# A decoder kernel: forget gate first, state space table on two engines, POOL's low angles before its high ones

## The reference

```
feat = x @ W_in; V, Q, F = split(feat)              # block 1, a gated recurrence over the 2 batches
V, Q = gelu(V), gelu(Q); lam = lb + (1 - lb) * sigmoid(F); K = 1 - lam
S_t = lam_t * S_(t-1) + K_t (x) V_t;  o_t = Q_t . S_t
x = layernorm(x + o @ W_out)
scores = (x @ Wq)(ctx @ Wk)^T / sqrt(32), 4 heads   # block 2
attn = softmax over the 32 largest of 154 scores;   c = mean over heads(attn) @ (ctx @ Wv)
u = layernorm(x) * (1 + g*scale_in(c)) + g*shift_in(c)
y = u convolved with K_l = 2 Re sum_n dC_n exp(dtA_n * l), l = 0..511   # s4d
y = y * (1 + g*scale_out(c)) + g*shift_out(c); h = x + y; h += ffn(layernorm(h)); layernorm
```

## Time and profile before

| | us |
|---|---|
| median of three runs | 663.56 (663.29 to 664.49) |
| the profiled execution, its own time | 663.11 |
| its span | 661.3 |
| PE busy | 603.2 (91%) |
| DVE busy | 439.0 (66%) |
| ACT busy | 287.9 (44%) |
| POOL busy | 246.5 (37%) |

### The profile page before, as it was taken

One profiled execution on the slowest core, in us unless ns is written; L12 is line 12 of the kernel. 1 busy time (PEld: TensorE's weight loads), 2 busy tenths in 40 slices (PEclk: granted clock), 3 DMA queues, 4 the chain that ended last, 5 costly groups with the idle time before them and its releaser, 6 DMA issues.

```text
span 661.3 us, 8811 instructions
## 1 busy us (share of the span) xinstructions
PE 603.2 (91%) x3171; PEld 302.0 (46%) x3172; DVE 439.0 (66%) x1173; ACT 287.9 (44%) x548; POOL 246.5 (37%) x179
## 2 busy tenths in 40 slices
PE   8864959998997999999999998999977999999997
PEld 4432548886572332222222442233622345556566
DVE  6899998556559846766776569668645675333335
ACT  7979968213230554444444333534232334221210
POOL 2899271422531344655465344557334100000001
PEclk9955879999999899999999999999979999999999
DMA  8300006021000000000000000000600000000001
GB/s 321 110 0 0 2 1 256 1 68 60 1 0 1 0 0 1 0 1 1 0 1 0 1 1 0 1 0 1 268 22 1 0 1 0 1 1 0 1 0 33
DMA packets 4945, 19.25 MB, mean 29 GB/s; under 512 B 2053, under 2 KB 3462, under 8 KB 4390
## 3 DMA queue, kind: packets, MB, share of 16 engines
q1 hardware_dynamic: 4902, 18.69, 7.5%
HBM read 18.16 MB, written 0.52 MB: 28 GB/s over the span
## 4 chain that ended last, share of the span: by engine, by line
PE 71%; DVE 14%; ACT 7%; POOL 4%; issue 4%; DMA 0%; POOLq 0%; DVEq 0%; ACTq 0%
PE PS L2401 11%; PE PS L1606 9%; PE PS L1622 8%; PE PS L2422 6%; PE PS L1564 5%; PE PS L1590 3%; PE PS L1692 2%; PE PS L1636 2%; PE PS L1609 2%; DVE SB L1853 2%; DVE SB L199 2%; PE PS L2091 2%; POOL SB L238 2%; ACT SB L468 1%; DVE SB L212 1%
## 5 line engine op out<-in xcount | busy, mean ns | idle before, releaser
L1853 DVE TENSOR_REDUCE SB<-PS 128x2 f32<-128x1024 f32 x64 | 78.4, 1226 | 62.9 <-PE PS L1590 62.8
L1839 POOL TENSOR_TENSOR SB<-SB 128x1024 f32<-128x1024 f32 x32 | 75.2, 2352 | 108.7 <-ACT SB L1791 107.8
L1791 ACT ACTIVATE SB<-PS 128x1024 f32<-128x1024 f32 x64 | 65.6, 1024 | 102.3 <-PE PS L1609 102.2
L2401 PE MATMUL PS<-SB 128*128 128x512 f32 x176 | 78.4, 594 | 0.0
L1606 PE MATMUL PS<-SB 64*128 64x512 f32 x256 | 70.4, 627 | 1.1 <-ACT SB L1795 1.1
L1622 PE MATMUL PS<-SB 128*64 128x512 f32 x256 | 67.6, 610 | 0.5 <-DVE SB L1885 0.5
L238 POOL TENSOR_TENSOR SB<-SB 128x4 f32<-128x4 f32 x18 | 19.3, 1073 | 116.9 <-DVE SB L204 104.3
L2460 ACT ACTIVATE SB<-PS 128x512 f32<-128x512 f32 x44 | 26.2, 597 | 80.2 <-PE PS L2401 78.8
L2486 DVE TENSOR_TENSOR SB<-SB,PS 128x512 f32<-128x512 f32 x44 | 30.0, 688 | 41.8 <-PE PS L2401 40.5
L1876 DVE RECIPROCAL SB<-PS 128x256 f32<-128x256 f32 x32 | 55.6, 1744 | 0.0
L2401 PEld LDWEIGHTS PS<-SB 128*128 128x128 f32 x176 | 32.2, 190 | 35.3 <-issue 33.7
(11 more groups left out here) (415 smaller groups left out, 1125.2 us busy)
## 6 DMA issues: line engine op xcount, KB each, us to landing
SB<-exp SPq DMA_DIRECT2D x1, 4352.0 KB, 14.1
SB<-moe SPq DMA_DIRECT2D x1, 4096.0 KB, 14.5
SB<-dft SPq DMA_DIRECT2D x1, 2304.0 KB, 11.6
SB<-att SPq DMA_DIRECT2D x1, 2048.0 KB, 8.2
SB<-mix SPq DMA_DIRECT2D x1, 768.5 KB, 4.4
SB<-mix SPq DMA_DIRECT2D x1, 640.0 KB, 5.5
SB<-ssm SPq DMA_DIRECT2D x1, 602.0 KB, 6.6
SB<-lat SPq DMA_DIRECT2D x1, 585.0 KB
```

Source lines behind the costliest of these rows:

```text
L1791: act.activation(expd[i % 2][:, 1024 * u:1024 * u + 1024], bank(2 * (u % 2), 2), ACT.Exp).then_inc(sem("d_exp"), 1)
L1839: pool.tensor_tensor(half_sums[half], e[:, 0:1024], e[:, 1024:], ALU.add).then_inc(sem("d_half_sum"), 1)
L1853: dve.tensor_reduce(shift[i % 2][:, qt:qt + DK + 1:DK], two_heads(bank(4, 2)), AX_X, ALU.max, negate=True)\
L2401: pe.matmul(bank(2 * (i % 3) + side), w, xsT[:, 512 * n:512 * n + 512], start=True, stop=True).then_inc(sem(("top2_w1", "top2_w3")[side]), 1)
```

## The change

In block 1 PE turns the first half of the stack (phases and rates) ahead of the features, and makes the features of the forget gate first; ACT takes the sigmoid first. DVE starts on the keys as soon as that is there. The table's last part (dC) goes from DVE to POOL as `b_pool_stack`, except the reciprocal; DVE copies the turned first half of the stack and writes eight of the 32 low phases itself. The statistics of the second half stand before the normalisation of the first. POOL's masks and powers come before its film weights. The second half's transposes stand on PE behind `score(0)`, the film inputs behind `score(1)`. The low rounding is in two halves, with `peak(0)` between; the high rounding stands behind the second pair's selection. The memset of 32x1024 is on DVE. POOL makes both low angles, then the marks and film rows, and then the high angles. ACT writes 14 of the 16 high phases behind the film inputs.

The diff, cut to its core:

```diff
--- before.py
+++ after.py
...
-        for m in range(3):
+        pe.wait_ge(sem("s_turns"), 2)
+        for i in range(2):
+            ins = pe.transpose(bank(7)[:, 128 * i:128 * i + 128], stack[:, 128 * i:128 * i + 128], ident)
+        ins.then_inc(sem("s_stack_turned"), 1)
+        for m in (2, 1, 0):
...
+            ins = pe.transpose(bank(7)[:, 128 * i:128 * i + 128], stack[:, 128 * i:128 * i + 128], ident)
+        ins.then_inc(sem("s_stack_turned"), 1)
 
     def a_act(act):
         b_act_stack(act)
         act.wait_ge(sem("a_features"), 2)
-        act.activation(gate_v, bank(0, 2), ACT.Gelu).then_inc(sem("a_gates"), 1)
+        act.activation(forget, bank(4, 2), ACT.Sigmoid, scale=-1.0).then_inc(sem("a_gates"), 1)
         act.wait_ge(sem("a_features"), 4)
         act.activation(gate_q, bank(2, 2), ACT.Gelu).then_inc(sem("a_gates"), 1)
         act.wait_ge(sem("a_features"), 6)
-        act.activation(forget, bank(4, 2), ACT.Sigmoid, scale=-1.0).then_inc(sem("a_gates"), 1)
...
         b_dve_stack(dve, follow)
         dve.wait_ge(sem("mix_in"), 16)
         follow(dve.tensor_scalar(one_less, mix["lower"], -1.0, 1.0, ALU.mult, ALU.add))
-        dve.wait_ge(sem("a_gates"), 3)
-
+        dve.wait_ge(sem("a_gates"), 1)
         follow(dve.tensor_scalar(keys, forget, one_less, None, ALU.mult))
+        follow(dve.scalar_tensor_tensor(carried[:, 0:512], keys[:, 512:], 1.0, keys[:, 0:512], ALU.subtract, ALU.mult))
+        dve.wait_ge(sem("a_gates"), 2)
         for n in range(2):
...
+        variances(0)
+        add(1)
+        spread(1)
+        norm_apply(dve, tiled(xsum), tiled(xs), 0).then_inc(sem("stage_half"), 1)
+        variances(1)
+        norm_apply(dve, tiled(xsum), tiled(xs), 1).then_inc(sem("stage_done"), 1)
 
 
...
+            ins = dve.tensor_copy(s[:, k, :], src)
+        ins.then_inc(sem("s_turns"), 1)
+        Ar, Ai = ssm["A_re"], ssm["A_im"]
+        dve.tensor_tensor(dt_(13), Ar, Ar, ALU.mult)
+        tt(dt_(14), Ai, Ai, ALU.mult)
+        tt(dt_(13), dt_(13), dt_(14), ALU.add)
+        dve.reciprocal(dt_(13), dt_(13)).then_inc(sem("s_dta"), 1)
+        dve.wait_ge(sem("s_stack_turned"), 1)
+        dve.tensor_copy(stack_T[:, 0:256], bank(7)[:, 0:256]).then_inc(sem("s_stack_in"), 1)
+        dve.wait_ge(sem("s_stack_in"), 1)
+        for l in range(LOW_ACT, LOW):
+            ins = dve.tensor_scalar(lag(low_r, LOW)[:, :, l], turn_T, float(l), ssm["quarter"], ALU.mult, ALU.add)
+        follow(ins)
...
+    def b_pool_stack(pool, follow):
+
+        tt = lambda o, a, b, op: pool.tensor_tensor(o, a, b, op)
+        s = stack.rearrange("p (k n) -> p k n", n=N_ST)
+        pool.wait_ge(sem("table_in"), 16)
+        pool.wait_ge(sem("s_trig"), 2)
...
-    def b_dve_rounds(dve):
-
+    def b_dve_low_rounds(dve, h):
+
+        c = slice(2048 * h, 2048 * h + 2048)
         dve.wait_ge(sem("s_low_products"), 1)
-        dve.tensor_scalar(low_k, low_r, MAGIC, MAGIC, ALU.add, ALU.subtract).then_inc(sem("s_rounds"), 1)
+        dve.tensor_scalar(low_k[:, c], low_r[:, c], MAGIC, MAGIC, ALU.add, ALU.subtract).then_inc(sem("s_rounds"), 1)
+
+    def b_dve_high_rounds(dve):
+
         dve.wait_ge(sem("s_high_turns"), 1)
         dve.tensor_scalar(high_t, high_r, MAGIC, MAGIC, ALU.add, ALU.subtract).then_inc(sem("s_rounds"), 1)
...
-        pool.wait_ge(sem("s_rounds"), 2)
+        pool.wait_ge(sem("s_rounds"), 3)
...
-        pool.wait_ge(sem("s_rounds"), 1)
+        pool.wait_ge(sem("s_rounds"), h + 1)
         pool.tensor_tensor(low_k[:, c], low_k[:, c], low_r[:, c], ALU.subtract).then_inc(sem("s_low_products"), 1)
...
+    def b_pe_turn(pe, half):
+
+        pe.wait_ge(sem("x_small_in"), 4)
+        if half == 0:
+            stay_warm(pe, 2, 0, ident)
+        pe.wait_ge(sem(("stage_half", "stage_done")[half]), 1)
+        for t in range(4 * half, 4 * half + 4):
+            ins = pe.transpose(PS[:, 2048 + 128 * t:2048 + 128 * t + 128], tiled(xs)[:, t, :], ident)
+        ins.then_inc(sem(("x_half_turned", "turned")[half]), 1)
+        if half == 0:
...
-        b_act_low_turns(act, 0, 24)
+        act.wait_ge(sem("s_stack_in"), 1)
+        b_act_low_turns(act, 0, 13)
...
-        b_act_low_turns(act, 24, LOW)
-        b_act_high_turns(act, 0, 10)
+        b_act_low_turns(act, 13, 20)
+        b_act_stack_in(act)
         act.wait_ge(sem("x_half_turned"), 1)
         act.activation(xsT[:, 0:512], bank(4), ACT.Copy).then_inc(sem("x_half_in"), 1)
-        b_act_high_turns(act, 10, HIGH)
+        b_act_low_turns(act, 20, LOW_ACT)
+        b_act_high_turns(act, 0, 2)
+
+    def b_act_turned(act):
+
         act.wait_ge(sem("turned"), 1)
...
+        b_pool_stack(pool, follow)
         pool.wait_ge(sem("small_in"), SMALL)
+        follow(pool.tensor_copy(mask_line, ctx_bytes))
+        follow(pool.tensor_scalar(mask_line, mask_line, 1.0, -NEG, ALU.subtract, ALU.mult))
+        by_batch = mask_line.rearrange("p (b g) -> p b g", b=B)
+        m2 = mask_low.rearrange("p (b h g) -> p b h g", b=B, h=2)
+        for h in range(2):
+            pool.tensor_copy(m2[:, :, h, :], by_batch)
+        pool_rstd_half(pool, 0)
+        pool.tensor_copy(ones_low, ones[0:1, :])
+        pool.memset(zeros_low, 0.0).then_inc(sem("masks_in"), 1)
+        pool_rstd_half(pool, 1)
         pool.wait_ge(sem("ssm_in"), 16)
         pool.tensor_scalar(film_w, ssm["W_film"], mod_gate, None, ALU.mult).then_inc(sem("film_w_in"), 1)
         pool.wait_ge(sem("film_w_in"), 1)
...
-        follow(pool.tensor_scalar(text_mask, text_mask, 1.0 / H_X, None, ALU.mult))
-        pool.wait_ge(sem("a_features"), 6)
-        pool.memset(attn1[96:128, :], 1.0).then_inc(sem("x_clear"), 1)
-        pool.wait_ge(sem("x_clear"), 2)
+        pool.tensor_scalar(text_mask, text_mask, 1.0 / H_X, None, ALU.mult).then_inc(sem("masks_in"), 1)
+        pool.wait_ge(sem("masks_in"), 2)
...
-        for t in range(4):
+        score(0)
+        b_pe_turn(pe, 1)
+        score(1)
+        b_pe_film(pe)
+        for t in (2, 3, 4):
             score(t)
-        score(4)
...
-        b_dve_rounds(dve)
+        b_dve_low_rounds(dve, 0)
         dve.wait_ge(sem("masks_in"), 1)
         peak(0)
+        b_dve_low_rounds(dve, 1)
         peak(1)
+        dve.memset(attn1[96:128, :], 1.0).then_inc(sem("x_clear"), 1)
         for j in range(PAIRS_X):
             if 0 < j < PAIRS_X - 2:
                 peak(j + 2)
             select(j)
             if j == 0:
                 peak(2)
+            if j == 1:
+                b_dve_high_rounds(dve)
             if j % 2 == 0:
                 selected(j)
             else:
...
         exponentials(0)
+        b_act_turned(act)
+        exponentials(1)
         scores_in(1)
         b_act_film_inputs(act)
-        exponentials(1)
+        b_act_high_turns(act, 2, HIGH)
         scores_in(2)
         exponentials(2)
...
+        b_pool_low_angles(pool, 0)
+        b_pool_low_angles(pool, 1)
         pool.wait_ge(sem("norm_rstd"), 2)
         b_pool_marks(pool, follow)
-        b_pool_low_angles(pool, 0)
+        b_pool_film_rows(pool, follow)
         b_pool_high_angles(pool)
-        b_pool_low_angles(pool, 1)
-        pool.wait_ge(sem("s_low_products"), 3)
-        b_pool_film_rows(pool, follow)
```

More of the change, by code:

```diff
@@ L326, in a_pe @@
             ins.then_inc(sem("a_out"), 1)
-            if half == 0:
-                b_pe_scorer(pe)
+        b_pe_scorer(pe)
+        pe.wait_ge(sem("s_stack"), 1)
+        pe.wait_ge(sem("s_stack_in"), 1)
+        for i in (2, 3):
+            ins = pe.transpose(bank(7)[:, 128 * i:128 * i + 128], stack[:, 128 * i:128 * i + 128], ident)
+        ins.then_inc(sem("s_stack_turned"), 1)
     def a_act(act):
@@ L336, in a_act @@
         act.wait_ge(sem("a_features"), 6)
[L337 removed]
+        act.activation(gate_v, bank(0, 2), ACT.Gelu).then_inc(sem("a_gates"), 1)
     def a_dve(dve, follow):
@@ L366, in add, with spread, variances @@
             dve.wait_ge(sem("a_out_read"), k + 1)
-        norm(dve, follow, tiled(xsum), tiled(xs), first_half="stage_half", prepare=add).then_inc(sem("stage_done"), 1)
+        def spread(k):
+            for t in range(4 * k, 4 * k + 4):
+                ins = dve.bn_stats(tiled(stats)[:, t, :], tiled(xsum)[:, t, :])
+            follow(ins)
+        def variances(k):
+            for t in range(4 * k, 4 * k + 4):
+                ins = dve.bn_aggr(moments.rearrange("p (t m) -> p t m", m=2)[:, t, :], tiled(stats)[:, t, :])
+            follow(ins)
+            dve.tensor_scalar(variance[:, 4 * k:4 * k + 4], moments.rearrange("p (t m) -> p m t", m=2)[:, 1, 4 * k:4 * k + 4],
+                              EPS, None, ALU.add).then_inc(sem("norm_variance"), 1)
+        add(0)
+        spread(0)
+        variances(0)
[4 more added lines that the diff above has]
+        norm_apply(dve, tiled(xsum), tiled(xs), 1).then_inc(sem("stage_done"), 1)
     Bf = Space(free_at, END)
@@ L442, in b_dve_stack @@
         tt(dt_(12), dt_(10), Ai, ALU.mult)
```

(20 more changed lines are left out.)

64 lines of the change are left out of this document (25 added, 39 removed).

## The result

The changed kernel is slower by half a percent. Sixteen runs have a median of 667.0 (665.34 to 671.08), sixteen of the kernel before on the same chip 663.61; the ratio is 1.0049, 95% interval [1.0027, 1.007]. The forecast was 667.7, with a range of 663.8 to 671.2. The profiled execution took 667.15 with a span of 665.3, 4.0 more than before.

A forecast was written before the change was run, and what follows sets the result against it. ACT's start of the high waves (T) was taken to set the end; POOL's queue with its rounding hindrances moves T from 45.28 to 49.5, so 663.11 + 4.2 = 667.3 profiled, 667.7 against the median; range 663.8 to 671.2.

The forecast's parts named there:

- T: Date at which ACT starts the three high waves, 45.28 before; forecast 49.5, moving the end one for one.
- The reserve of 5.8: POOL's high angles were ready at 39.5, 5.8 before ACT came for them; the change touches this.
- the first order: POOL's low half starts before DVE's second low rounding, which stands behind it; high angles end at 49.9.
- the second order: Second rounding slips in before POOL's low half; POOL loses 1.1 to each of three roundings; T 49.1 or 48.9.
- The terms: POOL's queue from 23.4: film weights 2.85 to 4.0, low halves 9.06, marks 1.3, film rows 4.5, high angles 4.5, gaps 0.2.
- The hindrance of the second rounding: DVE's second half rounding, due at 28.1, stands behind POOL's low half and runs 32.0 to 33.2.
- The first stage: Block 1: keys at 9.4 instead of 12.81, second variance at 22.3 instead of 24.07; gain must pass through T.
- Rival 3: New DVE memset also stands behind POOL's second low half: T +8.3, 671.9; chance 0.13.
- Rival 2: Gain and loss meet, POOL unhindered and some operation shorter: T within 1.3 of 45.28, 663.6; chance 0.06.
- Rival 4: PE idle longer before 57 keeps the low clock past 80: +1 to +2, 669; chance included in first case's 0.66.
- Rival 1: Reserve not used up, high angles ready before ACT: T 42.6, -2.7, 660.9; chance 0.10.
- the unhindered sum of 22.4: Lower sum of POOL's queue from 23.4 through the high angles, without DVE and POOL hindering each other: T 45.8.

The follow-up runs named there:

- experiment 2: Kernel before, with five or ten memsets on POOL between first low half and high angles: 664.22 (ratio 1.0013) and 668.12 (1.0076).
- experiment 5: Changed kernel, POOL's first low half waiting for both low roundings and film rows moved behind the high angles: 663.6, ratio 0.9995.
- experiment 1: Kernel before with only POOL's order changed (both low angles, film rows, then high angles): 667.12, ratio 1.0042.
- experiment 7: experiment 5 plus high rounding inside the second pair's selection, extra warming products on PE, and POOL's marks ahead of its low angles: 662.05, ratio 0.9978.

## Why the prediction was right, point by point

- **T sets the end, one for one.** Shown by experiments 2 and 5 and by the table, to within 0.8. The distance from T to the taps was 48.33 before, 48.04 after.
- **The reserve of 5.8 is used up by the order.** Shown by experiments 1 and 2.
- **T = 49.5.** Measured 49.42 in the first order (said: 49.9), 48.53 in the second (said: 48.9). ACT was ready at 48.0 and 43.6 (said: 48.3 and 42.6). Both orders occur, in one and the same program. The median moved 3.4 to 3.7 where 4.2 was forecast: T in most runs is probably the second order's, but only two executions were profiled, so that is argued.
- **The terms.** Film weights 4.1, 0.1 above the upper bound of 4.0: the first product of 128 took 1.50 beside DVE's rounding. Low halves 4.51 and 4.55, marks 1.2 for 1.3, film rows 4.5, high angles 4.54 for 4.5. The hindrance of the second rounding, said to last from 28.1 to 33.2, was 27.75 to 32.72. DVE's idle time before its sixth pair, said to be 3 or more, was 2.62 and 6.12 in the two profiles.
- **Right by luck: that the second rounding was held.** The prediction let four normalisations stand behind POOL's first film weights, 1.5 in all, until 26.1, and so ended the first rounding at 27.4. They took 1.68 for 1.12, a hold of 0.6, and the first rounding ended at 25.79. Only the late scores (next point but one) put the second rounding back to 27.75; in the second profile they came in time and it escaped. That cost the forecast nothing because the prediction had played both orders and found them 0.8 to 1.0 apart.
- **The first stage.** Keys at 9.00 (said 9.4); the products then waited 0.81 for a gelu, which I had not named; third sum's reader at 15.17 (15.4); second variance done at 21.86 (22.3), 2.2 before it was. POOL's small operations ended at 14.95, in the bound given (6.3, with DVE in the way up to 9) and before they were wanted.
- **What I had not seen.** The first peak waited 1.30 for its scores, because PE's clock stood at 0.50. It changed which order was played, not T by more than 0.9.
- **Two-input operations of DVE do hold POOL.** The prediction took the rule from the Trainium skill (SBUF — State Buffer, "Who interferes with whom") and thought that the rows showed less. They show it, on POOL's side. Its products of 64 columns, first while DVE was idle, then beside DVE's products, and those products beside POOL and without it:

```profile
L475 POOL TENSOR_TENSOR SB<-SB x2: 322/324/325, 10.7 to 11.0; 128x64 f32<-128x64 f32 x2
```
```profile
L475 POOL TENSOR_TENSOR SB<-SB x3: 651/767/777, 11.6 to 13.0; 128x64 f32<-128x64 f32 x3
```
```profile
L356 DVE TENSOR_TENSOR SB<-SB x2: 804/845/886, 11.3 to 12.1; 128x512 f32<-128x512 f32 x2
```
```profile
L365 DVE TENSOR_TENSOR SB<-SB x1: 693/693/693, 15.9 to 15.9; 128x512 f32<-128x512 f32 x1
```

(The three numbers are the shortest, median and longest duration in ns, then come the first and last start.) POOL took 0.65 to 0.78 for 0.32, DVE 0.80 to 0.89 for 0.69: 0.3 to 0.5 for POOL and 0.1 to 0.2 for DVE each time. In the kernel before it was the same: the products of line 350 took 0.69 and 0.95, which their mean of 0.78 hides. None of it reached T by way of POOL, which still idled 1.27 ahead of its first power; what DVE lost, 0.4 in three products, may stand in the date of the second variance.
- **The rivals.** Rival 3 fell with the memset's 0.91 beside the low half, and it took 0.91 in all nine profiles that have it. The Trainium skill (SBUF — State Buffer, "Who interferes with whom") says that a DVE instruction with at most one SBUF input and outside its two-port modes does not contend with GpSimd. A memset has no input, and the trace agrees. Rival 2 did not come: POOL was never unhindered. Rival 4 did not come as put: up to the last low rate the clock was even higher than before (0.75 against 0.64). A loss of its size (1.3) stood behind the taps instead, and was gone at the end of the span. Rival 1 did not come either: POOL's second power ended at 22.95, and with the unhindered sum of 22.4 that makes 45.4 for the high angles, behind ACT's 43.6. Experiment 5 comes nearest to it: with the film rows out of the way ACT waited 1.39.

## What to carry to other kernels

Before an operation moves on the engine that looks idle, find who is released by it and how early it is ready today: that reserve is the budget. Here the first 5.8 of delay cost nothing and what went beyond cost its full length. When a stage is made shorter, follow the gain to the next joint before counting it; a gain of 2.2 stood on DVE and ACT and none of it passed POOL. And place long operations of DVE and GpSimd against each other by their times: one moved "earlier" may come to stand behind the other for its whole length, and take its engine's queue with it.

## What the runs showed of the hardware

- A rounding on DVE (128x2048, one input in SBUF, two constants) takes 1.21 or 1.22 when it starts first or alone, 4.97 or 3.78 when POOL's 2048-column product had started before it. The other way round, POOL loses about 1.0 for each that comes in its way: a product of 128 columns takes 1.43 to 1.51 for 0.46. In these pairs the second stood until the first was through. It isn't so in all: four normalisations of DVE that started 0.04 behind POOL's operation over 512 columns (22.94, 1.57) took 1.68 for 1.12.
- A product of DVE with two inputs in SBUF (128x512) and POOL's products of 64 columns hold each other too: 0.65 to 0.78 for 0.32 on POOL, 0.80 to 0.89 for 0.69 on DVE.
- The delay is inside the second operation's busy time and is no "wait" in the profile. It is found by comparing one operation's durations, and a "gap" seen ahead of the next one may be that (experiment 7).
- Which operations are held: on DVE the tensor_scalar roundings (4.97) were, the memset (0.91) was not, both beside 2048-column products of POOL. The searches for the largest eight in the selection took 0.30 to 0.32 each beside them and with POOL idle.
- The granted clock at the first scores, from 24 to 32, was 0.50 (the level of 1.2 GHz) in two profiles and 1.00 in the others. The changed kernel had both: 0.50 with PE busy 1.95 of the 2.8 before 22.8, and 1.00 with PE busy 1.81 of them. What decided it isn't shown.
